# Routed blocks of a mixture-of-experts layer: the turn of the gated rows moved behind the next pair's token turn, down products one step later, three buffers instead of two

## What is computed

```python
x = x + attn(xn) + ffn(xn)
# attn: softmax(q k^T / 16) v for each of the 4 sequences, all 256 wide
# ffn: router softmax over 16 experts, the best two, their scores normalised
h = silu(xt @ We_gate.T) * (xt @ We_up.T)      # 128 wide, per expert
y = sum over the two chosen experts of score * (h @ We_down.T)
y = y + sigmoid(xt @ Wsg.T) * shared           # shared expert, 512 wide
```

## Time and profile before

| | us |
|---|---|
| median of 3 executions | 526.70 (526.47 to 526.92) |
| the profiled execution | 526.41 |
| its span in the trace | 524.4 |
| PE busy in the span | 515.1 (98%) |
| DVE / ACT / POOL busy | 403.7 / 281.2 / 173.8 |
| granted TensorE clock, mean | 0.997 of full speed |

### The profile page before, as it was taken

The page is one execution under the profiler, slowest core; times in us unless marked ns, Lnnn a source line. Parts: engine busy times, 40 slices in busy tenths (PEclk is TensorE's granted clock), DMA queues, the critical chain, the costliest instruction groups (busy, mean ns, idle before and its releaser), DMA issues.

```text
span 524.4 us, 10083 instructions
## 1 busy us (share of the span) xinstructions
PE 515.1 (98%) x3489; PEld 470.5 (90%) x3489; DVE 403.7 (77%) x839; ACT 281.2 (54%) x467; POOL 173.8 (33%) x162
## 2 busy tenths in 40 slices
PE   8999999999999999999999999999999999999997
PEld 6898988878888999999999896989999898989897
DVE  5889457898987686767775378996969879697985
ACT  4777775245655465555555448272737355363641
POOL 0001021011005777777750432433240606051500
PEclk9999999999999999999999999999999999999999
DMA  8927275111113555886595710711170302121111
GB/s 317 391 102 274 94 291 215 60 32 58 33 61 113 199 180 181 250 284 195 183 144 157 234 41 22 241 54 57 42 239 22 91 24 83 36 65 56 52 50 62
DMA packets 29888, 69.29 MB, mean 132 GB/s; under 512 B 5008, under 2 KB 9488, under 8 KB 28816
## 3 DMA queue, kind: packets, MB, share of 16 engines
q1 hardware_dynamic: 22496, 49.68, 26.2%
q0 software_dynamic: 6912, 18.88, 13.7%
q10 hardware_dynamic: 432, 0.09, 0.1%
HBM read 41.37 MB, written 27.26 MB: 131 GB/s over the span
## 4 chain that ended last, share of the span: by engine, by line
PE 86%; DVE 6%; issue 3%; ACT 2%; DMA 1%; POOL 0%; SPq 0%; DVEq 0%; POOLq 0%; ACTq 0%
PE ps L728 51%; PE ps L929 11%; PE ps L734 8%; PE ps L859 7%; PE ps L961 6%; PE ps L814 1%; DVE probs_f L1560 1%; ACT probs_f L1230 1%; DMA stage_gu<-in_shared 1%; PE ps L823 1%; DVE acc L1336 1%; DMA blk_x<-rows,row 1%; ACT scored_t L1045 1%; PE ps L876 1%; POOL blk_x L695 0%
## 5 line engine op out<-in xcount | busy, mean ns | idle before, releaser
L715 POOL DMA_INDIRECT rows_y<-ytab,slot x64 | 75.5, 1180 | 136.6 <-DVE acc L1575 120.3
L695 POOL DMA_INDIRECT blk_x<-rows,row x80 | 83.8, 1048 | 58.7 <-DVE row L1440 31.5
L728 PE MATMUL ps<-vv,pT 128*128 128x258 f32 x768 | 96.7, 284 | 0.0
L728 PE MATMUL ps<-xT,shared_w 128*128 128x512 f32 x384 | 94.2, 399 | 1.4 <-DVE sil L1317 1.4
L728 PEld LDWEIGHTS ps<-vv,pT 128*128 128x128 f32 x768 | 94.2, 189 | 0.5
L728 PEld LDWEIGHTS ps<-xT,shared_w 128*128 128x128 f32 x384 | 71.9, 191 | 16.8 <-issue 2.2
L728 PE MATMUL ps<-qT,xbT_hi 128*128 128x512 f32 x256 | 79.5, 392 | 1.0 <-ACT scored_t L1045 0.8
L929 PE MATMUL ps<-expert_w,blk_xT 128*128 x480 | 66.6, 288 | 0.2 <-issue 0.2
L929 PEld LDWEIGHTS ps<-expert_w,blk_xT 128*128 128x128 f32 x480 | 59.7, 190 | 0.6 <-issue 0.6
L728 PEld LDWEIGHTS ps<-qT,xbT_hi 128*128 128x128 f32 x256 | 47.2, 188 | 11.9 <-ACT scored_t L1045 2.0
L1230 ACT ACTIVATE probs_f<-probs_f 128x1024 f32<-128x1024 f32 x32 | 33.5, 1048 | 37.7 <-DVE probs_f L1560 37.7
(11 more groups left out here) (164 smaller groups left out, 859.2 us busy)
## 6 DMA issues: line engine op xcount, KB each, us to landing
ytab<-blk_y SPq DMA_DIRECT2D x40, 256.0 KB
keys<-xT SPq DMA_DIRECT2D x8, 1024.0 KB, 5.7
stage_e<-in_experts SPq DMA_DIRECT2D x16, 384.0 KB, 3.2
rows<-xn SPq DMA_DIRECT2D x8, 512.0 KB, 3.0
xbT_hi<-keys SPq DMA_DIRECT2D x8, 512.0 KB, 6.1
xbT_lo<-keys SPq DMA_DIRECT2D x8, 512.0 KB, 7.4
out<-acc SPq DMA_DIRECT2D x32, 128.0 KB, 1.7
acc<-in_x SPq DMA_DIRECT2D x7, 512.0 KB, 8.8
```

Of the source, the lines that this page charges most:

```text
L695: e.indirect_dma_start(out=blk_x[:, q, n, :], out_offset=None, in_=rows, in_offset=bass.IndirectOffsetOnAxis(ap=row[:, 2 * b + n:2 * b + n ...
L715: e.indirect_dma_start(out=rows_y[:, r, k, :], out_offset=None, in_=ytab, in_offset=bass.IndirectOffsetOnAxis(ap=slot[:, k, i:i + 1], axis=0),
L728: ins = e.matmul(dst, stationary(p, k), moving(q, k), start=(n == 0), stop=(n == total - 1))
```

## The change

At step b the order becomes GU(b), Down(b-3), Turn(b+2), Gather(b+4), HidT(b-1), then the other work and `bias_in`. The loop has one step more. `blk_hT` becomes three separate buffers (HR = 3): two lie where the two lay, the third in a part of the shared expert's weights that is no longer read by then. ACT's HI copy of `blk_hidden` b now waits for Down(b-3), and for b = 2, the first use of the new buffer, for the last down product of the shared expert. The number of instructions of each kind is the same as before.

```diff
+HR = 3
-    for b in range(PAIRS + 2):
+    for b in range(PAIRS + 3):
...
             steps.append(("blk_gate_up", b))
-        if 0 < b <= PAIRS:
-            steps.append(("blk_hidden", b - 1))
-        if b > 1:
-            steps.append(("blk_down", b - 2))
+        if b > 2:
+            steps.append(("blk_down", b - 3))
         if b + 2 < PAIRS:
             steps.append(("blk_turn", b + 2))
         if b + XR < PAIRS:
             steps.append(("blk_load", b + XR))
+        if 0 < b <= PAIRS:
+            steps.append(("blk_hidden", b - 1))
...
-        blk_hT = at("blk_hT", r_h + 4096, [P, 2, 2, 2 * P], F32R)
+        blk_hT = [at(f"blk_hT{n}", (r_h + 4096, r_h + 6144, r_w + 4 * 4 * KD * D + PART + 2048)[n], [P, 2, 2 * P], F32R)
+                  for n in range(HR)]
...
-                    if b >= 2:
-                        e.wait_ge(blk_downed, 2 * (b - 1))
-                    copied(blk_hT[:, r, HI, :], ps[:, 4 + r, 0:2 * P], blk_hT_hi)
+                    if b == HR - 1:
+                        e.wait_ge(downed, 4 * NCH)
+                    elif b >= HR:
+                        e.wait_ge(blk_downed, 2 * (b - HR + 1))
+                    copied(blk_hT[b % HR][:, HI, :], ps[:, 4 + r, 0:2 * P], blk_hT_hi)
```

More of the change, by code:

```diff
@@ L960, in tensor_program @@
                         for at, (p, q) in enumerate(PASSES):
-                            ins = e.matmul(ps[:, 6 + r, n * D:(n + 1) * D], blk_hT[:, r, p, n * P:(n + 1) * P],
+                            ins = e.matmul(ps[:, 6 + r, n * D:(n + 1) * D], blk_hT[b % HR][:, p, n * P:(n + 1) * P],
                                            weights(b, n, q, 2 * D, D), start=(at == 0), stop=(at == len(PASSES) - 1))
@@ L1477, in vector_program @@
                     e.wait_ge(blk_hT_hi, b + 1)
-                    remainder(blk_hT[:, r, LO, :], ps[:, 4 + r, 0:2 * P], blk_hT[:, r, HI, :], blk_hT_lo)
+                    remainder(blk_hT[b % HR][:, LO, :], ps[:, 4 + r, 0:2 * P], blk_hT[b % HR][:, HI, :], blk_hT_lo)
                 elif kind == "blk_down" and a[0] % 2 == 0:
```

## The result

| | before | changed |
|---|---|---|
| median of 9 executions, us | 526.58 | 527.84 |
| lowest to highest | 525.94 to 528.13 | 527.25 to 528.57 |
| the profiled execution | 526.41 | 527.48 |
| its span | 524.4 | 525.5 |

The ratio is 1.0022, with a 95% interval of 1.0014 to 1.0031. The changed kernel is slower by about 1.2 us (1.26 between the medians), twice the 0.6 us that was forecast (527.3 us), and inside the range given.

A forecast was written before the change was run, and what follows sets the result against it. The block stage was taken as bound by TensorE; +0.9 us (first steps), +0.1 (last steps) and -0.4 (seams between PE's groups) gave +0.6, so 527.3 us against a median of 526.70, range 526.0 to 528.5.

The forecast's parts named there:

- What bounds the kernel: Block stage: TensorE (PE) is the bound, busy for all of 57.56 us, with no wait to remove in 38 steady steps.
- the moved copies: Steady steps: `blk_hT` copies on ACT and DVE stand behind those of `blk_y` and `blk_xT`; costed at nothing.
- The first steps: Step 2: Turn(4) waits 1.09 us for its gather instead of 0.17, uncovered by HidT(1) and Down(0); loss 0.92 us.
- the gather is not late: Rival, first steps: Turn(4)'s 0.17 us are PE's own or the landing usually falls otherwise; 526.4 us, chance 0.2.
- The seams: Where PE's groups meet in 37 steady steps: -0.01 us each, -0.4 in all, bounds 0 and -0.8.
- signs of being wrong: Turn(4) at 177.0 without wait; steady distance 2.80 or more, or under 2.78; mid-stage waits for `blk_hT` or `blk_h`.
- part 2: Joins between PE's groups in steady steps: GU ending against Down -0.02 us, Down behind GU +0.01, so -0.01 a step.
- The rival that the seams cost nothing: Rival, steady steps: joins between PE's groups cost nothing in any order; +1.0 us, 527.7 us, chance 0.12.
- The last steps: From GU(39) to attention: 5.69 us against 5.58 unchanged, as late copies delay Down(38) and Down(39); loss 0.1, bounds -0.3 and +0.4.
- The sequencer's case: Rival, steady steps: PE's address work loses its cover with 18 matmuls in a row; 528.8 or 529.9 us, chance 0.1.
- The rival of a larger gain: Rival: GU(18)'s unexplained 0.4 us wait may go and the joins between groups give 0.8; down to 525.6 us, chance 0.08.

The follow-up runs named there:

- f4: The changed kernel with Down(b-2) at step b, so that only HidT moves; 544.84 us, ratio 1.0351 to the kernel before.
- f2: The changed kernel with SP's three weight loads held back, each for one of Turn(4), Turn(5), Turn(6); 527.93 us, ratio 1.0016 to the kernel before.
- f3: The changed kernel with HidT(b-1) back behind GU(b), so only the down products come a step later; 527.84 us, ratio 1.0017 to the kernel before.
- g1: The kernel before, unchanged, run once more on chip 8; 526.59 us.
- g2: The changed kernel, unchanged, run once more on chip 8; 527.94 us, ratio 1.0019 to the kernel before.
- e4: The kernel before with SP's three weight loads held back, on chip 10; 549.53 us, ratio 0.9996 to the kernel before there.
- e1: The changed kernel, unchanged, run once more on chip 10; 546.78 us, ratio 0.9941 to the kernel before there.

## Why the prediction was right, and where it was not

**What bounds the kernel, and the moved copies: right.** PE is the bound in every steady step, there was no wait to remove, and the copies that ACT and DVE now do in another order hold nobody up: no wait for `blk_hT` or `blk_h` in the steady steps. f4 shows what is missing without the later Down, 0.5 us a step.

**The first steps: right in mechanism, a little small.** Forecast 0.92, with a bound of 0.93; measured 1.24 and 0.88. The wait was forecast to end at 178.0, it ended at 178.37 and 178.25. The bound assumed that the gather lands at the same time in both executions; in the traces without pauses, f2 left aside, Turn(4) starts between 177.9 and 178.7, 4.0 to 4.5 us behind the issue of its gather, while GU(1) moves by up to 0.7. In the first pair the distance was 4.16 before and 4.48 after, and that 0.3 is what the loss of 1.24 lies over the forecast. That 0.92 lies between the two measured losses is therefore in part luck. A slip of 0.04 is in the working: a Turn that had to wait takes 0.39 and not 0.43 (178.04 to 178.43), so that GU(3) would start at 178.64 and not at 178.68; the 0.92 does not rest on it. The cause, SP's loads beside it, was only inferred from the queue's 86.1% and the shorter distance of pair 1; f2 shows it, with 3.14 us against 4.0 to 4.5, and also that after holding the loads back PE waits for a later gather. The rival "the gather is not late" falls with it.

**The seams: wrong, by 0.66 us.** Of the signs of being wrong one was met, a steady distance of 2.80 or more. The step that failed is the composition of part 2: -0.02 for a GU that ends against a Down and +0.01 for the Down behind it were both read, at a resolution of 0.01 us, from groups in other surroundings, and added. GU did shrink from 1.44 to 1.42; but Down grew from 0.72 to 0.73 and HidT from 0.21 to 0.22, the turns stand no closer, and the sum is +0.007 a step instead of -0.01. f3, with the old order of groups, is back at 2.799. The rival that the seams cost nothing was nearer (0 instead of +0.26), and its 527.7 was the closest figure of all. The Trainium skill's rule of a fixed cost per matmul (TensorE: Matmul & The Clock Gate, section "Wait — 56ns, not 53.3ns?"), which I read as holding whatever the neighbours, is closer to these runs than my sum was, without being exact: the same 24 instructions take 2.800 or 2.807 us by their order.

**The last steps: right within 0.1.** Forecast +0.1, measured 0.0. Down(38) came 3.66 us behind GU(39) and not 3.85, because consecutive operations of DVE overlap in the profile by about 0.08 us, which I had added up end to end: the copy of `blk_y` of 36 starts at 284.40, before the 284.06 + 0.42 at which `blk_h` ends, and the next operation at 285.00, before that copy's end at 285.08. Down(39) came at 4.86 and not 4.97: on ACT the copy for `blk_hT` starts at 285.79, 0.11 before that of `blk_y` ends, and the 4.97 was mis-added, since 3.98 + 0.41 + 0.42 + 0.14 is 4.95.

**The sequencer's case: no sign of it.** 18 matmuls with a computed address in a row leave no gap of half a matmul. A part of it, less than 0.01 us a step, could be in the 0.007; nothing here tells.

**The rival of a larger gain: half of it happened, by chance.** The idle time at GU(18) was gone in the profiled execution of the changed kernel, which took 0.46 us off the difference of the two traces. But g1 is without it too, in the old order, and g2 has one of 0.76.

So the mechanism held. The difference came out at 1.26 us instead of 0.6, mostly by the seams, whose sign was wrong (0.66 of it); the first steps add 0.3 in one pair of traces and nothing in the other. Attention started 1.05 us later than before in the first pair, where 0.6 was forecast. No measurable change was given 0.67 and slower 0.22; the interval of the ratio, 1.0014 to 1.0031, straddles the 0.2% that were said to be the limit of what can be told.

## What to carry to other kernels

In a stage whose one engine never waits, look at its first steps before you reorder: a group of work that covers nothing in the steady state may be all that covers a landing there, and moving it costs about its length, here 0.9 to 1.2 us for 0.93. Do not take a seam's price from rows with the resolution of the price itself; seventeen steps in one stretch give it seventeen times finer, and even so a seam belongs to its surroundings: have the new order measured before you count on it. Slack that bought nothing in two sessions was worth 3 us in a third, on another chip, so a kernel is better timed on more than one.

## What the runs showed of the hardware that was not expected

Chips of one kind ran the same program 4% apart (526.6 to 526.7 us in three sessions, two of them on chips 0 and 8, and 549.9 on chip 10), all at a granted clock of 0.99 of full speed or more. All runs on chip 10 were taken in one session, so whether this belongs to the chip or to that session is open. Attention takes 238.0 us on either, and almost the whole difference is in the block stage (it ends at 310.85 us in e4 and at 286.42 in the first trace). There, on the slower chip, ACT stands still for about 2 us in every second step with its inputs ready (once in e4, in two pieces in e1), under a releaser that had long been done. The changed order was 0.6% faster there and 0.2% slower elsewhere. PE itself has single idle times of 0.4 to 0.8 us with no releaser, none to two per trace, in both kernels, all between GU(17) and GU(20). The DMA engines are busy to 0.97 there (222 to 224 us, first trace), but to 1.01 in the four us before and 1.02 in the four behind, where PE does not stop, and to 0.95 in the same place of g1, which has no such idle time; so their load alone does not make it, and the cause is open. A difference of 1 us between two single traces can be made of such idle times alone.

The rows of a gather were usable 3.0 to 3.3 us after the start of POOL's issue for pair 1, ahead of SP's three loads, and after at most 3.14 us for pair 4 where these loads were held back (f2); with the 0.77 MB of loads issued beside it, pair 4 took 4.0 to 4.5 us.
